# Sparse output experts: the last pair's sorted results moved into the next batch, and each chunk of results read by ScalarE and VectorE

## The reference

```python
gates = sigmoid(x @ w_gate)                    # 8 heads x 8 experts per token
sel = argmax(gates, axis=-1)                   # one expert per head and token
gm = one_hot(sel) * gates
values = einsum('bhne,ehdk,bnd->bhnk', gm, value_experts, x)
attn = softmax(causal(q @ k.T))
out = attn @ values                            # 64 wide per head
out = einsum('bhne,ehkd,bhnk->bhnd', gm, output_experts, out)   # sparse: one expert per head and token
return out.sum(axis=1)                         # over the 8 heads
```

## Time and profile before

| | |
|---|---|
| median of 3 runs | 2146.98 us (2142.21 to 2147.06) |
| the profiled execution, its own time | 2155.61 us |
| its span in the trace | 2153.8 us, 29336 instructions |
| PE busy | 1934.9 us (90%) |
| DVE busy | 1250.2 us (58%) |
| ACT busy | 980.3 us (46%) |
| POOL busy | 729.6 us (34%) |
| blocks A and B of the four batches | about 170 to 1150 us of the span |

### The profile page before, as it was taken

The page is one execution under the profiler, slowest core; times in us unless marked ns, Lnnn a source line. Parts: engine busy times, 40 slices in busy tenths (PEclk is TensorE's granted clock), DMA queues, the critical chain, the costliest instruction groups (busy, mean ns, idle before and its releaser), DMA issues. The chain is left out here.

```text
span 2153.8 us, 29336 instructions
## 1 busy us (share of the span) xinstructions
PE 1934.9 (90%) x10024; PEld 1024.5 (48%) x10024; DVE 1250.2 (58%) x2553; ACT 980.3 (46%) x1899; POOL 729.6 (34%) x660
## 2 busy tenths in 40 slices
PE   8989897988888888889998999999999999986993
PEld 5666344744456444565563333343343333335772
DVE  5434752266522665239877767778777877742342
ACT  3412242212323123222105879778877887861220
POOL 4330143104433054211106133224632541326575
PEclk9999998989989999899998999999999999997997
DMA  8741156214633046351125374337542643105997
GB/s 284 208 161 56 56 180 196 87 42 118 195 116 120 27 129 189 97 168 51 55 31 134 80 243 114 64 68 176 113 107 39 174 79 49 50 26 181 267 193 164
DMA packets 184077, 262.88 MB, mean 122 GB/s; under 512 B 48135, under 2 KB 140117, under 8 KB 182648
## 3 DMA queue, kind: packets, MB, share of 16 engines
q1 hardware_dynamic: 121208, 179.21, 30.9%
q0 software_dynamic: 26624, 47.18, 8.8%
q10 hardware_dynamic: 36096, 34.61, 4.9%
HBM read 165.92 MB, written 104.44 MB: 126 GB/s over the span
## 5 line engine op out<-in xcount | busy, mean ns | idle before, releaser
L2623 ACT ACTIVATE d_prob<-ps 128x512 f32<-128x512 f32 (+1 forms) x832 | 473.5, 597 | 155.2 <-PE ps L2473 154.4
L2650 DVE CUSTOM_DVE_ANT_0 ps<-ps,maskN 128x801 f32<-128x801 f32 x480 | 467.6, 1015 | 125.6 <-PE ps L2443 125.4
L1056 PE MATMUL ps<-vx_or_keys,b_xT 128*128 128x512 f32 x512 | 253.5, 623 | 19.1 <-DVE val_or_prob L1511 18.9
L2485 PE MATMUL ps<-d_prob,vaug 128*32 128x512 f32 (+1 forms) x1664 | 225.9, 609 | 0.3 <-ACT d_prob L2623 0.3
L692 POOL DMA_INDIRECT val_or_prob<-sorted_out,oxB x96 | 98.7, 1028 | 359.6 <-DVE xx L1637 160.7
L2472 PE MATMUL ps<-maskT,identb 128*128 128x512 bf16 (+1 forms) x498 | 192.0, 385 | 4.4 <-POOL maskT L2347 2.5
L2619 ACT CAST ps<-maskT 128x512 f32<-128x512 bf16 (+1 forms) x310 | 185.5, 598 | 0.0
L265 POOL DMA_INDIRECT table<-xr,slot x128 | 128.4, 1004 | 168.4 <-PE ps L2473 133.2
L1350 ACT ACTIVATE prob_or_gate<-ps,b_mx 128x512 f32<-128x512 f32 (+3 forms) x128 | 66.1, 525 | 187.8 <-DVE b_mx L1502 185.8
L1511 DVE TENSOR_TENSOR val_or_prob<-ps,b_gm 128x512 f32<-128x512 f32 x128 | 88.2, 689 | 103.4 <-PE ps L1056 101.6
L1056 PEld LDWEIGHTS ps<-vx_or_keys,b_xT 128*128 128x128 f32 x512 | 92.1, 195 | 114.1 <-issue 79.1
(11 more groups left out here) (356 smaller groups left out, 3153.7 us busy)
## 6 DMA issues: line engine op xcount, KB each, us to landing
sorted_out<-og_or_pT ACTq DMA_DIRECT2D x90, 256.0 KB
oxB<-in_B_ox SPq DMA_DIRECT2D x264, 64.0 KB
c_rawT<-in_maskT SPq DMA_DIRECT2D x24, 512.0 KB
vx_or_keys<-k_parts SPq DMA_DIRECT2D x60, 200.1 KB, 7.1
k_parts<-x_k SPq DMA_DIRECT2D x16, 600.4 KB
table<-xr POOLq DMA_DIRECT2D x16, 578.0 KB
e_buf<-table SPq DMA_DIRECT2D x32, 289.0 KB, 4.0
oxB<-sorted_in SPq DMA_DIRECT2D x12, 704.0 KB, 5.4
```

What stands on the lines that cost most here:

```text
L1056: mm = pe.matmul(ps[:, bank, :], xTB[:, c, t * P:(t + 1) * P], vxB[:, c, h, :], start=c == 0, stop=c == NC - 1)
L2485: mm = pe.matmul(ps[VW * h:VW * (h + 1), ACC, :], vaug[0:w, G % 2, i, h, :], prob[0:w, T % 2, h, :], start=i == 0, stop=i == NKT - 1)
L2623: nc.scalar.activation(prob[0:w, T % 2, h, :], ps[0:w, BANKS[GH * T + h], :], ACT.Exp, scale=SCALE_C).then_inc(exped, 1)
L2650: v.tensor_tensor_reduce(banks, banks, maskN[:, t, MO[half]:MO[half] + w], 1.0, -3.0e38, ALU.add, ALU.max, mp[:, t, h, half:half + 1]).the ...
```

## The change

1. `place`: pieces 0 and 1 stay before pair 0 (after units 3 and 5). Pieces 2, 3 and 4 move into `sorted_pair(b, 0)` on VectorE: piece 2 after the last `turned_b`, piece 3 after unit 10, piece 4 after `write_rows`. The second set of addresses (`from_sorted`) is gone, so `placed` counts 21 per batch.
2. The last pair's groups and chunks (Q = 4b - 1) move, for b = 1 and 2, from `sorted_between` into `sorted_pair(b, 0)`, at the same places as in the other pairs. For b = 3 `sorted_between` stays.
3. In `last_pair` chunks 4 and 5 of pair 4b + 2 are taken out and put into the next batch's attention A at i = 1, before and after the scores; the rest is reordered.
4. Each chunk is read in halves: ScalarE bank 6 (first head), VectorE bank 7 (second head, `read_second`); the next chunk waits for both. Chunks of `sorted_between` are still read by ScalarE alone.
5. The two heads' results stand side by side in `sorted_out`: one DMA for each chunk, with 2 KB runs, in place of two with 1 KB runs.
6. `gather` of pairs p < 3 fetches two tiles before the scatter and two after it; `add_back` of tiles 2 and 3 moves one pair later. `keep_x` moves from p = 1 to p = 2.

```diff
@@ SyncE @@
-                        if p == 1 and b >= 1:
+                        if p == 2 and b >= 1:
                             keep_x(b - 1)
@@ GpSimd @@
+                        ahead = 2 if p + 1 < PAIRS else NT
+                        if Q >= 2:
+                            gather(Q - 2, range(ahead))
                         scatter(b, p)
+                        if Q >= 2:
+                            gather(Q - 2, range(ahead, NT))
@@ TensorE, attention A @@
+                    if b and i == 1:
+                        out_sorted(PAIRS * b - 2, 4)
                     if i < NT and (b == 0 or i >= 1):
                         for j in range(NKC):
                             scores(b, i, j)
+                    if b and i == 1:
+                        out_sorted(PAIRS * b - 2, 5)
 ...
                 if before >= 0:
                     pe.wait_ge(blocks_a, before + 1)
+                    pe.wait_ge(blocks_v, min(before + 1, CHUNKS * (EARLIER - 1)))
 ...
+                if p == 0 and b < SORTED:
+                    pe.wait_ge(placed, PLACING * b + 13)
@@ TensorE, sorted_pair: each of these once per group and chunk @@
-                if p:
+                if Q:
                     turn_sorted(Q - 1, 0)
@@ TensorE, the order of the batches @@
-                if b:
+                if b == SORTED:
                     sorted_between(b)
@@ ScalarE, attention A @@
+                    if b and i < 2:
+                        read_blocks(PAIRS * b - 2, 4 + i)
@@ ScalarE, read_blocks @@
+                if c == 0 and not between:
+                    act.wait_ge(placed, PLACING * ((Q + 1) // PAIRS + 1))
 ...
+                    nc.scalar.copy(o[:, 0:w, 0], ps[:, bank, 0:w * D].rearrange("p (j n) -> p j n", n=D)).then_inc(blocks_a, 1)
+                    act.wait_ge(blocks_v, n + 1)
@@ VectorE @@
+            def read_second(Q, c):
+                n = CHUNKS * Q + c
+                v.wait_ge(blocks_mm, n + 1)
+                if n >= 2:
+                    v.wait_ge(kept[c % 2], 16 * (n // 2))
+                if c == 0:
+                    v.wait_ge(placed, PLACING * ((Q + 1) // PAIRS + 1))
+                w = min(2, BLOCKS - 2 * c)
+                v.tensor_copy(outS[1][c % 2][:, 0:w, 1], ps[:, 7, 0:w * D].rearrange("p (j n) -> p j n", n=D)).then_inc(blocks_v, 1)
@@ VectorE, sorted_pair @@
+                if p and Q >= 3:
+                    add_back(Q - 3, 2)
+                    add_back(Q - 3, 3)
+                if p == 0:
+                    place(b, 2)
                 weigh(b, p)
                 maxima(b, p + 1, 0)
                 unit(b, u + 2)
-                add(0)
+                if p == 0:
+                    place(b, 3)
+                if Q >= 2:
+                    add_back(Q - 2, 0)
                 unit(b, u + 3)
                 write_rows(b, p)
-                add(1)
+                if Q >= 2:
+                    add_back(Q - 2, 1)
+                if p == 0:
+                    place(b, 4)
                 unit(b, u + 4)
+                if Q:
+                    read_second(Q - 1, 0)
                 maxima(b, p + 1, 1)
 ...
```

More of the change, by code:

```diff
@@ L43 @@
 CHUNKS = -(-BLOCKS // 2)
-PLACING = 23
+PLACING = 21
 HC, DC = 16, 16
@@ L456, in attentions_ab @@
     zeroed, scattered, gathered = k.rows_zeroed, k.rows_scattered, k.rows_gathered
-    (numbers, picked, counted, placed, weighted, rows_mm, rows_v, sorted_mm, sorted_a, blocks_mm, blocks_a, added,
+    (numbers, picked, counted, placed, weighted, rows_mm, rows_v, sorted_mm, sorted_a, blocks_mm, blocks_a, blocks_v, added,
      ld_sorted) = (
@@ L679, in scatter, with gather @@
                             bounds_check=2 * ROWS - 1, oob_is_err=True).then_inc(scattered[Q % 2], 16)
-            def gather(Q):
+            def gather(Q, tiles):
                 b, p = divmod(Q, PAIRS)
                 all_kept(g, Q + 1)
-                for t in range(NT):
+                for t in tiles:
                     n = NT * Q + t
@@ L918, in turn_b @@
                     pe.wait_ge(gated, EB * (Q - EARLIER - 1) + 7 + g)
-                if g == 0 and p == 0 and b < SORTED:
-                    pe.wait_ge(placed, PLACING * b + 13)
-                if g == 0 and p >= 2 and b < SORTED:
+                if g == 0 and p and Q >= 2 and b < SORTED:
                     pe.wait_ge(sorted_a, 3 * (Q - 1))
@@ L973, in out_sorted @@
             def out_sorted(Q, c):
-                b, p = divmod(Q, PAIRS)
-                bank = 6 if p < PAIRS - 1 or c % 2 == 0 else 0
+                b, between = (Q + 1) // PAIRS, Q + 1 == EARLIER
+                bank = 0 if between and c % 2 else 6
                 if c == 0:
@@ L1360, in read_sorted @@
             def read_sorted(Q, g):
-                if g == 0 and Q % PAIRS < PAIRS - 1:
-                    act.wait_ge(placed, PLACING * (Q // PAIRS + 1))
                 act.wait_ge(sorted_mm, 3 * Q + g + 1)
@@ L1399, in attention_b @@
                     Q, more = PAIRS * b + p, p + 1 < PAIRS
-                    behind = p >= 1 and b < SORTED
+                    behind = Q >= 1 and b < SORTED
                     read_turned(Q)
@@ L1422, in attention_b @@
                         probabilities(b, p + 1, 2)
-                    if behind:
+                    if behind and more:
                         for c in range(4, CHUNKS):
@@ L1475, in attention_a @@
                         turned_probabilities(T - 1, 0)
+                    if b and i == 1:
+                        read_second(PAIRS * b - 2, 4)
                     if i < NT:
@@ L1485, in attention_a @@
                                         ALU.mult).then_inc(bias, 1)
+                    if b and i == 1:
+                        read_second(PAIRS * b - 2, 5)
                     if 1 <= i <= NT:
@@ L1600, in place @@
                     v.tensor_tensor(end_block, first_block, n, ALU.add).then_inc(placed, 1)
-                    v.wait_ge(placed, at + 20)
+                    v.wait_ge(placed, at + 18)
                     wide = [P, HB, BLOCKS, EB]
@@ L1677, in attention_b @@
                 if b:
-                    all_kept(v, PAIRS * b)
-                def placing(piece):
-                    if b < SORTED:
-                        place(b, piece)
+                    all_kept(v, PAIRS * b - 1 if b < SORTED else PAIRS * b)
                 unit(b, 0)
@@ L1687, in attention_b @@
                 unit(b, 3)
-                placing(0)
+                if b < SORTED:
+                    place(b, 0)
                 unit(b, 4)
-                placing(1)
                 maxima(b, 0, 2)
                 unit(b, 5)
-                placing(2)
+                if b < SORTED:
+                    place(b, 1)
                 unit(b, 6)
-                placing(3)
                 unit(b, 7)
-                placing(4)
                 if b + 1 == NB:
@@ L1822, in last_pair @@
                 weigh(b, p)
+                if Q >= 3:
+                    add_back(Q - 3, 2)
+                    add_back(Q - 3, 3)
                 add_back(Q - 2, 0)
                 write_rows(b, p)
-                for t in range(1, NT):
-                    add_back(Q - 2, t)
+                read_second(Q - 1, 0)
+                add_back(Q - 2, 1)
+                for c in range(1, 4):
+                    read_second(Q - 1, c)
+                add_back(Q - 2, 2)
+                add_back(Q - 2, 3)
             def ending_pair(b):
```

137 lines of the change are left out of this document (74 added, 63 removed).

## The result

| | before | after |
|---|---|---|
| median of 4 runs | 2147.02 us (2142.21 to 2151.10) | 2173.31 us (2166.47 to 2182.54) |
| ratio, 95% interval | | 1.0126 (1.0081 to 1.0172) |
| profiled execution, its own time | 2155.61 us | 2170.13 us |

The change makes the kernel slower by 1.3%. The prediction was 2160.4 us, range 2138 to 2180, slower with a chance of 0.68. The direction and the mechanism hold. A second set of runs of the same two kernels, on another occasion, gave 1.011 (1.0081 to 1.0138), with 1.008 to 1.017 expected.

A forecast was written before the change was run, and what follows sets the result against it. TensorE, busy 90% of the span, was taken as the bound, so its waits around blocks A and B decide. The terms summed to +13.4 us on the 2146.98 median: 2160.4 us, range 2138 to 2180.

The forecast's parts named there:

- (a): Pair 1's first sorted group starts later after T0, unit 8's start: late placing delays its rows' load, +50.0 us.
- (b): Head of block B: unit 8 starts 1.3 us sooner, no longer behind piece 2, three times: -3.9 us.
- (d): Gates to unit 8 in batches 1 and 2: the clock recovers without the serial stretch, -5.7 us.
- (c): The serial stretch `sorted_between` of batches 1 and 2 goes away and nothing takes its place: -31.9 us.
- (e): Last pair: the next batch's first transposes start 5.3 us sooner, VectorE becoming the late engine, three times: -15.9 us.
- VectorE is the new bound in the last pair: Rival, chance 0.15: `read_second` waits for matmuls, tiles 1 to 3 behind it, so no gain there: +15.9, 2176 us.
- (f): Chunks 4 and 5 in attention A: context products wait for chunk 5's copy, in batch 2 also GpSimd: +19.4 us.
- (h): Restart after the waits for sorted rows: TensorE's matmuls run slower, 1.9 us, three times: +5.4 us.
- (i): Halved chunk copies in the pairs: 0.5 us saved in each of six pairs, -3.0 us.
- SyncE is in time: Rival, chance 0.08: SyncE's 22 loads don't hold up the sorted rows: +10.2 in place of +50.0, 2115 us.
- Gains and losses cancel: Rival, chance 0.22: last pairs gain -8 each, pairs -1.5 each, no restart: -6, 2141 us, with half of that 2150.
- The change does not do what it says: Rival, chance 0.10: chunk halves are never read at once, pairs 1 us longer each: +9, 2169 us.

The follow-up runs named there:

- cheap loads: The changed kernel with each expert load taking a fixed expert, so SyncE reads no register: 2130.37 us, 0.9929 of the kernel before.
- the kernel with both repairs: The changed kernel with all placing before pair 0 and ScalarE's half of chunk 5 copied before tile 1's exponential in attention A: 2120.23 us, 0.9874.
- early chunk 5: The changed kernel with ScalarE's half of chunk 5 copied before tile 1's exponential in attention A: 2280.33 us, 1.0043, on the slower chip.

## Why the prediction was right, step by step

*(a), the term that decides.* Right in mechanism and place, and shown by four kernels: removing the late placing (45 us off), putting it alone into the kernel before (49 us on), cheap loads (39 us off), and moving one load (only 12 us to be had). Its size was 4.9 us short, nearly all in batches 1 and 2. In batch 0 the placing ended at T0 + 20.7, predicted 20. In batch 1 it ended at T0 + 22.6, predicted 21.7, and its 22 loads took 29.91 us where I used batch 0's 27.57 for all three; the group started 3.0 us later than forecast there, 1.4 in batch 2 and 0.5 in batch 0. "SyncE itself catches up" was right for the kernel after (one wait of 1.69 us in a later pair), but only because TensorE loses its time in pair 1 already; the two kernels that moved the rows' load show the chain over two pairs behind it.

*(b) and (d), 2.5 us short.* In batches 0 and 1 they are right (-1.5 and -4.2, predicted -1.3 and -4.0). In batch 2 the clock did not recover. The windows from the gates to unit 8 (length, busy PE, PEld, DVE, ACT, POOL, granted clock, DMA, GB/s), b = 1 and 2:

```profile
439.15:475.24 36.09, 33.59 (x119) 15.76 (x119) 24.85 (x45) 7.17 (x21) 4.26 (x4) 1.00 0.05 15
704.44:743.85 39.41, 36.91 (x118) 17.97 (x118) 24.82 (x45) 7.17 (x21) 6.69 (x7) 0.91 0.13 34
```

The failed step is "the rows agree, 0.92 after the stretch with waits and 1.00 without": three rows in which both happened to fall together. In batch 2 there is no serial stretch any more, and the clock is 0.91 and the stretch 3.3 us longer than batch 1's. That batch 1's term came out as forecast is then luck too. The section on the hardware has more such stretches.

*(c), exact.* 437.25 to 439.15 is 1.90 us, as in batch 0. Nothing took its place.

*(e), -15.9 for -15.9, for a slightly other reason.* VectorE became the late engine, as said. But it is not the gather of tile 3 alone that holds it. The end of batch 1's last pair, VectorE and ScalarE:

```profile
621.91 0.69 DVE L1671 COPY og_or_pT<-ps 128x512 f32<-128x512 f32 x1 [2.20 <-DMA sorted_out<-og_or_pT]
622.51 1.86 DVE L1661 TENSOR_TENSOR kS<-kS,val_or_prob 128x256 f32<-128x256 f32 x4
...
626.59 1.60 ACT L1341 ACTIVATE val_or_prob<-ps,a_mx 128x1601 f32<-128x1601 f32 x1 [4.11 <-DVE a_mx L1507]
```

`read_second` 3 waits 2.20 us for the DMA of chunk 1, and the last two adds stand behind it. So the rival "VectorE is the new bound in the last pair" described the mechanism, and only its price was wrong. In batch 2 the gain was 2.5 where I had 5.3, in the other two 6.7 and 6.8: the sum is right by two errors that cancel.

*(f), +20.7 for +19.4.* The context products wait for ScalarE's copy of chunk 5, 3.32 us in all three batches, and behind it take 5.44 us in place of 3.74; batch 2 has the wait for GpSimd too. Predicted 5.1, 9.2, 5.1, measured 6.4, 8.4, 5.9. The slower products, 1.7 us, were not in the sum.

*(g), small, as said.* -1.4 for -1.0.

*(h), there, and a part of it counted twice.* From pair 1's first sorted group to its second TensorE does the same work in every kernel. With the early placing it takes 5.9 us at a clock of 1.00 in all three batches. In the kernel after it takes 7.65, 8.98 and 8.64 us, at 0.76, 0.64 and 0.67. But in the kernel before it took 5.94, 7.59 and 7.59: in batches 1 and 2 the shorter waits there, 3.33 and 3.70 us, had their restart already. Batch 1, before and after (the columns are those of the earlier trace rows):

```profile
515.72:523.31 7.59, 7.58 (x31) 3.01 (x31) 3.36 (x5) 2.04 (x5) 0.00 (x0) 0.78 0.31 86
...
534.28:543.26 8.98, 8.98 (x30) 3.60 (x31) 3.35 (x5) 2.03 (x5) 0.00 (x0) 0.64 0.20 58
```

The difference over three batches is +4.2 us (+1.9 in the trace of the second set), where the prediction took 1.9 us for each batch as new, 5.4.

*(i), the right size for a reason not shown.* Behind that stretch the pairs are 2.9 us shorter than before, predicted -3.0; with (h)'s +4.2 that is the row's +1.2. The kernel with whole copies has half of it, 1.5 us, without any halves, and its time is the same. So the halves show as 1.4 us in these traces, and what gives the rest is open.

*The rivals.* "SyncE is in time" had the right rule: the kernel with cheap loads meets its condition (15.4 us for loads, below the break-even of 23.1) and comes out faster than before, 0.9929. Its time, 2130, is 15 over the 2115 given, and most of that is (a) itself. The rival gave it +10.2, with pair 1's group 1 us early in batch 0; by (a)'s own terms loads of 16 us bring that group to T0 + 20 + 16 + 1.6 + 5.0 = T0 + 42.6 (1.6 being what the 29.2 us hold besides the loads), 5.1 us late, and being early would need loads of about 10 us. Measured are T0 + 41.0, 48.4 and 48.0, +21.1 in all. "Gains and losses cancel" has no support in any row. "The change does not do what it says" is right that the halves bring nothing, and its price, pairs longer by 1 us each, is not there.

## What to carry to other kernels

Before an instruction is moved to a later place "because its engine is idle there", follow the semaphore that it raises: here 2.3 us of VectorE work, moved by 17 to 19 us, started 22 register-addressed loads late, and pair 1's first sorted group came 17 to 20 us later in every batch. Ask of a queue that only issues how long its work takes from its first release to the one transfer that is needed; if that is longer than the distance to the consumer, moving one transfer ahead mostly moves the wait (12 of 45 us gained here), and what helps is an earlier release or cheaper issues. Splitting a copy over two engines gained nothing here, where the second half stands behind the other engine's own work. And before a clock or a wait is put in a sum as new, look whether the kernel before pays it already.

## What the runs showed of the hardware that was not expected

*The clock in a stretch with nothing unusual before it.* The stretch from the gates to unit 8 is the same work in batches 0, 1 and 2. In the nine traces of the changed kernel and its variants on the chips where the kernel before takes 2147 us, the granted clock in it was 0.91 or 0.92 in 9 of 27 cases and 0.99 or 1.00 in the others, in any batch, with a clock of 1.00 or 0.99 in the 20 us before each. In all nine low cases the loss lies at the start of the stretch: the mean over its first 6.8 us is 0.50 to 0.55, which is the lower of TensorE's two levels for nearly all of it, and the mean behind that is 0.99 or 1.00. Batch 2 of the kernel after, the stretch's start and its rest:

```profile
704.44:711.24 6.80, 6.80 (x20) 4.83 (x21) 2.66 (x4) 0.38 (x1) 5.66 (x6) 0.50 0.58 148
711.24:743.85 32.61, 30.11 (x99) 13.14 (x97) 22.16 (x42) 6.79 (x20) 1.03 (x1) 1.00 0.03 10
```

In the 1.9 us ahead of it TensorE does eight transposes and waits 0.83 us, at a clock of 1.00, and it does exactly that in batch 1 too, where the clock stays at 1.00. Even batch 0, which I had taken as the undisturbed case, falls once (in the kernel with both repairs). It costs 3.0 to 3.3 us where it happens. What decides it, no run here shows; one should not build a term on it from three rows.

*Nearly half of a register-addressed load is the register.* 1.24 us per load with the expert's number read from memory, 0.70 us with a fixed address, same bytes.

*What these waits cost besides themselves is the clock.* The same 32 products take 3.74 us with no wait before them and 3.81 behind a wait of 1.56 us, both at a granted clock of 1.00. Behind a wait of 3.32 us they take 5.44 us, and the clock is 0.69; 3.74 / 0.69 is 5.42, so the clock explains all of it. The length of the wait alone does not decide: unit 8's four matmuls take 1.98 us behind a wait of 2.88 us in the kernel before, and 3.41 behind one of 2.52 in the kernel after. The 32 products behind 1.56 us (early chunk 5) and 3.32 us (the kernel after):

```profile
410.44:414.25 3.81, 3.81 (x34) 3.81 (x35) 0.45 (x1) 1.24 (x2) 0.00 (x0) 1.00 0.67 214
...
642.86:648.30 5.44, 5.43 (x32) 5.24 (x32) 0.00 (x0) 0.00 (x0) 3.33 (x3) 0.69 0.13 48
```

*Stops of three engines on one chip.* On one chip the kernel before took 120 us more and 22 expert loads 31 to 38 us, where they take 27 to 30 on the others. In the kernel with the early placing ScalarE's copies of chunks stood 14 times, 86.6 us in all, for a releaser that the trace calls remote, while GpSimd went on issuing in the one shown above; the same kernel on the other chip has no such row. The change with the early placing is 0.9955 there and 0.9900 here. Why that chip is slower, and whether these stops are its cause or a part of it, stays open.
